# Self-attention's first stretch of a fused four-layer kernel, in halves of 512 tokens: second projection in two other banks, value products moved up, rows of ones filled by ScalarE

## What is computed

```python
def _mha(xk, xv, xq, Wk, Wv, Wq, Wo, bo, masked):        # 16 heads of 16
    K = jnp.einsum('bse,hed->bhsd', xk, Wk)
    V = jnp.einsum('bse,hed->bhsd', xv, Wv)
    Q = jnp.einsum('bqe,hed->bhqd', xq, Wq)
    scores = jnp.einsum('bhqd,bhkd->bhqk', Q, K)
    scores = jnp.where(causal, -jnp.inf, scores)
    att = jax.nn.softmax(scores / jnp.sqrt(sk), axis=-1)
    out = jnp.einsum('bhqk,bhkd->bhqd', att, V)
    ...
x = x + tanh(g_xattn[2]) * _L2_xattn_ref(_layernorm(x), ctx, ...)   # a = _mha(inputs, inputs, inputs, ..., masked=True) first
```

## Time and profile before

| | us |
|---|---|
| median of 3 runs | 2710.25 |
| lowest, highest | 2708.65, 2712.22 |
| the profiled execution | 2702.28 |
| its span, first to last instruction | 2700.5 |
| self-attention's stage begins | 1039.4 |
| its first peak product | 1078.75 |
| its maxima turned (L3168) | 1092.1 |
| first unit of batch 0 (L3235) | 1096.0 |

### The profile page before, as it was taken

One profiled execution on the slowest core, in us unless ns is written; L12 is line 12 of the kernel. 1 busy time (PEld: TensorE's weight loads), 2 busy tenths in 40 slices (PEclk: granted clock), 3 DMA queues, 4 the chain that ended last, 5 costly groups with the idle time before them and its releaser, 6 DMA issues. The chain is left out here.

```text
span 2700.5 us, 43042 instructions
## 1 busy us (share of the span) xinstructions
PE 2420.3 (90%) x12786; PEld 1429.2 (53%) x12787; DVE 1612.7 (60%) x3262; ACT 1288.6 (48%) x2559; POOL 1351.7 (50%) x2270
## 2 busy tenths in 40 slices
PE   6997999999996775799999999899969975999997
PEld 3554666766663553344445344355546663666664
DVE  5884664655554874687877868488866644212121
ACT  4664443544443773466566566566653431222221
POOL 3665663233445774224353434466875304656663
PEclk9998999999998998899999999999988986999999
DMA  4001000000100003222141231100004151222222
GB/s 137 6 1 67 1 0 1 1 0 1 47 1 16 1 0 76 62 66 71 31 111 44 54 87 37 48 24 24 1 1 164 47 197 24 45 46 47 43 47 28
DMA packets 85449, 115.14 MB, mean 43 GB/s; under 512 B 15432, under 2 KB 64432, under 8 KB 83600
## 3 DMA queue, kind: packets, MB, share of 16 engines
q1 hardware_dynamic: 66736, 92.36, 11.4%
q0 software_dynamic: 18528, 20.50, 4.7%
HBM read 77.92 MB, written 34.64 MB: 42 GB/s over the span
## 5 line engine op out<-in xcount | busy, mean ns | idle before, releaser
L3411 ACT ACTIVATE L2S_pT<-L2S_t_ps 128x512 f32<-128x512 f32 (+3 forms) x768 | 356.2, 491 | 212.8 <-PE L2S_t_ps L3235 204.3
L3475 DVE TENSOR_REDUCE L2S_mx<-L2S_s_ps 128x1 f32<-128x768 f32 (+7 forms) x384 | 350.5, 951 | 111.0 <-PE L2S_s_ps L3158 110.2
L3235 PE MATMUL L2S_t_ps<-L2S_q,L2S_k 98*128 98x512 bf16 (+3 forms) x768 | 248.4, 334 | 16.3 <-DMA L2S_q<-L2S_mrow 6.4
L3715 POOL TENSOR_SCALAR_AFFINE_SELECT L2S_pT<-L2S_pT 128x128 f32<-128x128 f32 x512 | 150.8, 309 | 170.0 <-ACT L2S_pT L3411 165.6
L3157 PE MATMUL L2S_s_ps<-L2S_k,L2S_q 96*128 96x512 bf16 (+3 forms) x768 | 198.5, 331 | 16.3 <-DVE L2S_mx L3475 7.5
L622 POOL TENSOR_TENSOR L_prob<-L_prob,L_rc 128x616 f32<-128x616 f32 x64 | 82.2, 1285 | 231.5 <-DVE L_rc L555 231.5
L4091 DVE TENSOR_TENSOR L3B_h<-L3B_si,L3B_u_ps 128x512 f32<-128x512 f32 x71 | 48.9, 688 | 237.4 <-PE L3B_u_ps L4034 237.4
L4008 POOL DMA_INDIRECT out<-L3B_y,L3F_rows x71 | 114.7, 1616 | 134.6 <-DVE L3B_y L4097 120.1
L3235 PEld LDWEIGHTS L2S_t_ps<-L2S_q,L2S_k 98*128 98x128 bf16 x768 | 72.8, 97 | 194.9 <-ACT L2S_pT L3411 129.0
L3335 PE MATMUL L2S_o_ps<-L2S_pT,L2S_v 128*32 128x512 f32 (+3 forms) x1536 | 165.4, 504 | 0.0
L319 PE MATMUL L_scores<-weights,L_xT 128*128 128x308 f32 x512 | 143.2, 423 | 2.3 <-ACT L_xT L442 1.6
(11 more groups left out here) (540 smaller groups left out, 5803.0 us busy)
## 6 DMA issues: line engine op xcount, KB each, us to landing
qk_parts<-L2S_part SPq DMA_DIRECT2D x90, 128.0 KB, 2.4
L2S_q<-qk_parts SPq DMA_DIRECT2D x32, 192.0 KB, 3.4
L2S_k<-qk_parts SPq DMA_DIRECT2D x30, 192.0 KB, 3.4
L2S_q<-qk_parts SPq DMA_DIRECT2D x32, 128.0 KB, 3.2
L3F_w<-in_L_gu SPq DMA_DIRECT2D x8, 512.0 KB, 6.9
weights<-in_L_w SPq DMA_DIRECT2D x8, 512.0 KB, 9.0
out<-x_sb SPq DMA_DIRECT2D x8, 512.0 KB, 3.3
expert_rows<-L_xn SPq DMA_DIRECT2D x8, 512.0 KB, 3.0
```

The source lines that it names most:

```text
L3235: nc.tensor.matmul(o[:, lo:512], k6[:, q % 2, j, kt * P:(kt + 1) * P], q6[:, q % 2, c, j, lo:512], start=True, stop=True).then_inc(s["t_fu ...
L3411: nc.scalar.activation(pT[:, st % SLOTS, j, lo:512], t_ps[j % 2][:, lo:512], ACT.Exp, scale=SK).then_inc(s["exp_done"], 1)
L3475: nc.vector.tensor_reduce(dst, src, AX.X, ALU.max).then_inc(s["mx_done"], 1)
L3715: nc.gpsimd.affine_select(out=edge, in_=edge, compare_op=ALU.is_ge, fill=0.0, base=0, pattern=[[1, P]], channel_multiplier=-1).then_inc(s[ ...
```

## The change

- `turn_x`, and `project(m)` for both m, go by halves c of 512 tokens: PE turns tiles 0 to 3 when these four are normalised, then tiles 4 to 7; ACT copies halves; PE projects, in this order, low queries, low keys, high queries, high keys, each half into one bank; ACT and DVE split halves (128x512 in place of 128x1024, twice as many).
- The second projection (m = 1) goes to `o_ps` (queries) and `r_ps` (keys), which nobody else uses yet, so it no longer waits for `s_ps`. Its low halves are made before the first peak, its high halves after peaks 2 and 3. `turn_max` on PE now also waits until the last rest has left `r_ps`.
- `first_v` of tiles 0 to 3 comes ahead of the second projection; tiles 4 and 5 come after peaks 0 and 1, tiles 6 and 7 after peaks 4 and 5.
- SP writes the low queries of quad 0, then of quad 1; when quad 0's have landed it reads them back, and then writes the low keys of quad 1 and the high queries. The high queries of quad 0 and quad 1's queries and keys are read later. POOL writes quad 0's low keys and reads them back as soon as these three have landed; then it writes the high keys of both quads and reads the high half back. Quads 0 and 1 take 24 writes of half the size in place of 12.
- The rows of ones in `k6` are filled by ACT as its first instruction in the stage, in place of POOL.
- ACT overwrites a high part of m = 0 in a half only when that half's writes have landed. `rest_done`, `act_pre` and `pre_full` are counted anew.

Names of semaphores and their setup are left out of the diff, and context lines.

```diff
@@ -2987,12 +2987,21 @@
...
-    turn_x()
-    project(0)
-    project(1)
+    for c in range(2):
+        turn_x(c)
+    for c in range(2):
+        for f in range(2):
+            project(0, c, f)
+    for t in range(4):
+        first_v(t)
+    for f in range(2):
+        project(1, 0, f)
     for n in range(TB):
         peak(0, n)
-        first_v(n)
+        if n in (2, 3):
+            project(1, 1, n - 2)
+        if n in (0, 1, 4, 5):
+            first_v({0: 4, 1: 5, 4: 6, 5: 7}[n])
...
@@ -3038,6 +3047,9 @@
...
+def projected(m, c, f):
+    return (o_ps, r_ps)[f][:] if m else s_ps[f][:, c * 512:(c + 1) * 512]
+
...
@@ -3086,14 +3098,35 @@
...
-        write(0, 0, 0, 2)
+        lows, highs = part[:, 0, :, lowc], part[:, 0, :, highc]
+        sp.wait_ge(s["split_low"], 1)
+        for qq, sem in ((0, "q_first"), (1, "q_rest")):
+            for p in range(3):
+                sp.dma_start(dram["parts"][0:1, qq, p, :, :, lowc].rearrange("o d h s -> (o d) h s"),
+                             lows[64 * qq:64 * qq + 64, p, :]).then_inc(s[sem], 16)
+        sp.wait_ge(s["q_first"], 48)
+        chip.settle(sp)
+        load(0, 0, "q", lowc, s["loaded_low0"])
+        sp.wait_ge(s["split_low"], 2)
+        for p in range(3):
+            sp.dma_start(dram["parts"][1:2, 1, 2 - p, :, :, lowc].rearrange("o d h s -> (o d) h s"),
+                         part[64:128, 1, p, lowc]).then_inc(s["k_rest"], 16)
+        sp.wait_ge(s["split_done"], 2)
+        for p in range(3):
+            for qq in range(2):
+                sp.dma_start(dram["parts"][0:1, qq, p, :, :, highc].rearrange("o d h s -> (o d) h s"),
+                             highs[64 * qq:64 * qq + 64, p, :]).then_inc(s["written0"], 16)
+        sp.wait_ge(s["written0"], 96)
+        chip.settle(sp)
+        load(0, 0, "q", highc, s["loaded_high0"])
+        sp.wait_ge(s["q_rest"], 48)
+        for n in ("k_first", "k_rest"):
+            sp.wait_ge(s[n], 48)
         sp.wait_ge(s["k_written"], 96)
         sp.sem_inc(s["written1"], 96)
-        written(0, 0)
-        for q in range(2):
-            for cols, n in ((lowc, "low"), (highc, "high")):
-                for which in "qk" if q else "q":
-                    load(0, q, which, cols, s[f"loaded_{n}{q % 2}"])
+        for cols, n in ((lowc, "low"), (highc, "high")):
+            for which in "qk":
+                load(0, 1, which, cols, s[f"loaded_{n}1"])
...
@@ -3168,28 +3201,27 @@
...
-        def turn_x():
-            pe.wait_ge(s["xn_done"], TB)
+        def turn_x(c):
+            pe.wait_ge(s["xn_done"], 4 * c + 4)
             for dh in range(KD):
-                for i in range(TB):
+                for i in range(4 * c, 4 * c + 4):
...
-        def project(m):
-            if m == 0:
-                pe.wait_ge(s["act_pre"], 2)
-            else:
-                pe.wait_ge(s["rest_done"], 2)
-            for f in range(2):
-                for c in range(2):
-                    for k in range(KD):
-                        mm = nc.tensor.matmul(s_ps[f][:, c * 512:(c + 1) * 512], w[("L2S_Wq", "L2S_Wk")[f]][:, k, m * P:(m + 1) * P],
-                                              xT[:, k, c * 512:(c + 1) * 512], start=(k == 0), stop=(k == KD - 1))
-                mm.then_inc(s["pre_full"], 1)
+        def project(m, c, f):
+            if not m:
+                pe.wait_ge(s["act_pre"], 2 * c + 2)
+            elif c:
+                pe.wait_ge(s["rest_done"], 5 + f)
+            o = projected(m, c, f)
+            for k in range(KD):
+                mm = nc.tensor.matmul(o, w[("L2S_Wq", "L2S_Wk")[f]][:, k, m * P:(m + 1) * P],
+                                      xT[:, k, c * 512:(c + 1) * 512], start=(k == 0), stop=(k == KD - 1))
+            mm.then_inc(s["pre_full"], 1)
...
-                pe.wait_ge(s["act_pre"], 6 + t // 2 - 1)
+                pe.wait_ge(s["act_pre"], 9 + (t - 4) // 2)
...
@@ -3205,12 +3237,13 @@
...
+            pe.wait_ge(s["rest_done"], 8)
...
-        pe.wait_ge(s["act_pre"], 10)
+        pe.wait_ge(s["act_pre"], 16)
...
@@ -3375,24 +3408,27 @@
...
-        def turn_x():
+        nc.scalar.activation(k6[KR:MR].rearrange("p a h s -> p (a h s)"), wide(chip.neghalf[KR:MR, 0:1], [MR - KR, 8 * S]), ACT.Copy,
+                             scale=0.0, bias=1.0).then_inc(s["k_ones"], 1)
+
+        def turn_x(c):
             for f in range(2):
-                act.wait_ge(s["pre_full"], f + 1)
-                copy(xT[:, f, :], s_ps[f][:], "act_pre")
-
-        def project(m):
-            for f in range(2):
-                act.wait_ge(s["pre_full"], 2 * m + f + 3)
-                if m:
-                    act.wait_ge(s[f"written{f}"], m * 96)
-                copy(part[:, f, 0, :], s_ps[f][:], "act_pre")
+                act.wait_ge(s["pre_full"], 2 * c + f + 1)
+                copy(xT[:, f, c * 512:(c + 1) * 512], s_ps[f][:, c * 512:(c + 1) * 512], "act_pre")
+
+        def project(m, c, f):
+            act.wait_ge(s["pre_full"], (5, 11)[m] + (2, 3)[m] * c + f)
+            if m:
+                for n, count in (((("q_first", 48), ("q_rest", 48)), (("k_first", 48), ("k_rest", 48))), ((("written0", 96),), (("k_written", 96),)))[c][f]:
+                    act.wait_ge(s[n], count)
+            copy(part[:, f, 0, c * 512:(c + 1) * 512], projected(m, c, f), "act_pre")
...
-                act.wait_ge(s["pre_full"], 7 + g)
+                act.wait_ge(s["pre_full"], (9, 10, 13, 16)[g])
...
@@ -3509,18 +3545,15 @@
...
-        def project(m):
-            for f in range(2):
-                n = 2 * m + f + 1
-                dve.wait_ge(s["act_pre"], 3 + 2 * m + f)
-                dve.wait_ge(s["split_done"], n)
-                nc.vector.tensor_tensor(first_rest[:, f, :], s_ps[f][:], part[:, f, 0, :], ALU.subtract).then_inc(s["rest_done"], 1)
-                dve.wait_ge(s["rest_done"], n)
-                if m:
-                    dve.wait_ge(s[f"written{f}"], m * 96)
-                nc.vector.tensor_copy(part[:, f, 1, :], first_rest[:, f, :]).then_inc(s["mid_done"], 1)
-                dve.wait_ge(s["mid_done"], n)
-                nc.vector.tensor_tensor(part[:, f, 2, :], first_rest[:, f, :], part[:, f, 1, :], ALU.subtract).then_inc(s["split_done"], 1)
+        def project(m, c, f):
+            n = 4 * m + 2 * c + f + 1
+            cols, mid, split, number = slice(c * 512, (c + 1) * 512), ("mid_low", "mid_done")[c], ("split_low", "split_done")[c], 2 * m + f + 1
+            dve.wait_ge(s["act_pre"], (5, 11)[m] + (2, 3)[m] * c + f)
+            nc.vector.tensor_tensor(first_rest[:, f, cols], projected(m, c, f), part[:, f, 0, cols], ALU.subtract).then_inc(s["rest_done"], 1)
+            dve.wait_ge(s["rest_done"], n)
+            nc.vector.tensor_copy(part[:, f, 1, cols], first_rest[:, f, cols]).then_inc(s[mid], 1)
+            dve.wait_ge(s[mid], number)
+            nc.vector.tensor_tensor(part[:, f, 2, cols], first_rest[:, f, cols], part[:, f, 1, cols], ALU.subtract).then_inc(s[split], 1)
...
@@ -3677,27 +3710,32 @@
...
-            nc.gpsimd.memset(k6[KR:MR], 1.0).then_inc(s["k_ones"], 1)
-            pool.wait_ge(s["k_ones"], 1)
...
-        def project(m):
-            if m:
+        def project(m, c, f):
+            if m or not f:
                 return
-            pool.wait_ge(s["split_done"], 3)
+            cols = slice(c * 512, (c + 1) * 512)
+            pool.wait_ge(s[("split_low", "split_done")[c]], 2 + c)
             chip.settle(pool)
-            for p in range(3):
-                for qq in range(2):
-                    nc.gpsimd.dma_start(dram["parts"][1:2, qq, 2 - p, :, :, :].rearrange("o d h s -> (o d) h s"),
-                                        part[64 * qq:64 * qq + 64, 1, p, :]).then_inc(s["k_written"], 16)
-            pool.wait_ge(s["k_written"], 96)
+
+            def k_out(qq, sem):
+                for p in range(3):
+                    nc.gpsimd.dma_start(dram["parts"][1:2, qq, 2 - p, :, :, cols].rearrange("o d h s -> (o d) h s"),
+                                        part[64 * qq:64 * qq + 64, 1, p, cols]).then_inc(s[sem], 16)
+
+            k_out(0, ("k_first", "k_written")[c])
+            if c:
+                k_out(1, "k_written")
+                pool.wait_ge(s["k_written"], 96)
+            else:
+                pool.wait_ge(s["k_first"], 48)
             chip.settle(pool)
             src = dram["parts"][1:2]
-            for cols, n in ((slice(0, S // 2), 0), (slice(S // 2, S), 1)):
-                for slot, count, p in ((0, 3, 0), (3, 2, 1), (5, 1, 2)):
-                    nc.gpsimd.dma_start(k6[slot * HD:(slot + count) * HD, 0, :, cols],
-                                        src[:, 0, p:p + count, :, :, cols].rearrange("o p d h s -> (o p d) h s")).then_inc(s[f"k_loaded{n}"], 16)
+            for slot, count, p in ((0, 3, 0), (3, 2, 1), (5, 1, 2)):
+                nc.gpsimd.dma_start(k6[slot * HD:(slot + count) * HD, 0, :, cols],
```

(1 more changed line is left out.)

6 lines of the change are left out of this document (3 added, 3 removed).

## The result

The changed kernel takes 2697.38 us (median of 8 runs, 2694.89 to 2702.51). The kernel before took 2707.57 beside it (median of 8, 2704.50 to 2712.22). The ratio of the two kernels is 0.9969, 95% interval 0.9959 to 0.9979: 8.4 us less, between 5.7 and 11.1. The two medians lie 10.2 us apart. The forecast was 2703.1 with a range of 2699.5 to 2707.5. Its sign was right; the measured time lies 2.1 us under the range.

What follows compares the result with a forecast made beforehand. The bound was the serial chain from the stage's beginning through the keys' write and read to the peaks: 10.5 us gained, 3.3 lost, 7.1 by the turned maxima. Off the 2710.25 median this gave 2703.1, range 2699.5 to 2707.5.

Steps and rivals of the forecast that it cites:

- The chain is thus xn, PE, ACT, DVE, a write, a read, PE: Stage beginning to first peak: a serial path without parallel work, so each microsecond saved there counts in the whole time.
- POOL's first write: Quad 0's low keys: POOL begins writing near 1058.0 us, with the stage beginning at 1039.4; before, 1065.21.
- DVE's order at the peaks: Among quad 0's peaks: peak 2, high queries' split, peak 3, high keys' split, then peaks 4 to 7.
- The rule on small transfers: Quad 0's writes: about 2.0 us fixed each, so halving them buys nothing; landing halved with bytes would gain 1.2 us more.
- the difference is taken off the median: 2703.1: Whole kernel: the gain of 7.1 us taken off the median of the runs shown, 2710.25 us.
- I take 4.4, the middle: Third read of quad 0's low keys: landing between bounds of 3.4 and 5.4 us, first peak at 1068.3.
- The stretch is 16.7 us in place of 13.4: First peak to turned maxima: two half splits on DVE and the half clock lose 3.3 us, bounds 1.5 and 5.
- From turned maxima to the first unit nothing changes, 3.9 us: The maxima's way through POOL after the peaks: 3.9 us as before, no loss.
- The late read: Rival, chance 0.18: keys' read lands in about 8 us, first peak 1072, gain 3.6, time 2706.6.
- The fill was not slow: Rival, chance 0.05: ACT's fill of ones takes 14 us, 5.3 late, gain 1.8, time 2708.4.
- Batch 0's first 30 us: Slower rival, chance 0.05: clock at 0.50 after the first unit loses 4 to 12 us; 2715 at 12.
- Splits hidden, clock full: Rival, chance 0.12: half splits slip under PE, full clock at the peaks; loss 0 to 1, gain 10, 2700.2.

Runs made afterwards that it cites:

- e8_late_keys: Changed kernel, but POOL writes no keys until all four halves are split, then writes all nine pieces before reading back; 2706.92 us, ratio to the kernel before 0.9997.
- e7_whole_norm: Changed kernel, but PE starts its first four transposes only when all eight tiles are normalised; 2698.97 us (one run).
- six variants named under e7: Six variants of the changed kernel with early transposes, a late clock rise and no fill on POOL; POOL's first write at 18.8 to 19.1 us after stage start.
- e12: The changed kernel itself measured once more, nothing altered; 2696.41 us (12 runs), ratio to the kernel before 0.9972.
- e11_reads_together: Changed kernel, but SyncE reads quad 0's low queries back only when POOL's low-key writes have landed, so both reads start together; 2698.84 us (one run).
- e5_splits_late: Changed kernel, but the second projection's high halves and their splits stand behind quad 0's turned maxima; 2694.53 us (5 runs), ratio to the kernel before 0.9948.
- e10: e5_splits_late, but SyncE also holds quad 1's high-half reads until quad 0's turned maxima have landed; 2691.61 us (9 runs), ratio to the kernel before 0.9947.
- e4: Changed kernel, but SP holds back the twelve writes of quads 2 and 3 until the two rows of maxima have landed; 2695.60 us (one run).
- e1: Changed kernel, but POOL fills the rows of ones again after the norm, as before; 2702.45 us (one run).

## Why the prediction was right and where it failed

**Right: the path and the order of things.** "The chain is thus xn, PE, ACT, DVE, a write, a read, PE": e8_late_keys shows its write and read, e7_whole_norm its beginning. One reading in it was incomplete: before, the queries' read ended PE's wait, 0.5 us behind the keys'. The steps, forecast against measured: ACT's fill 7.0 and 7.02; POOL's first write S+18.6 and S+17.7 (S+18.8 to 19.1 in the six variants named under e7); last write's issue to the first read's 3.5 and 3.4 (1060.89 to 1064.25); DVE's order at the peaks as written, with peak 3 between the splits.

**The rule on small transfers.** Writes of 64 KB landed in 2.1 us (three of SyncE's, 1059 to 1062 us) and 2.3 us (POOL's), where one of 128 KB took 2.5. Half the bytes saved 0.2 to 0.4 us, not 1.2. The Trainium skill, page "DMA: Bandwidth & Descriptors", section "Anatomy of one DMA — SWDGE (gpsimd) path", has it so for transfers that POOL issues, with about 2.0 us fixed; this trace agrees (2.3 us for POOL's, where the estimate was 2.15). Six of SyncE's writes of 64 KB beside POOL's low reads, issued from 1064 to 1067 us, took 3.1 us.

**Failed: the base.** The step "the difference is taken off the median: 2703.1" took 2710.25, a median of 3 runs, for the kernel's time. It was 2707.57, 2707.84 and 2707.16 in groups of 8 to 20 runs (the first group holds the three), some 2.7 us lower. The measured 2697.38 lies 5.7 us under the forecast: 2.7 of these are the base, and 3.0 the gain, which was 7.1 in the forecast and is 10.2 between the two medians (10.8 in e12). By the ratios the gain is 8.4 and 7.6 us, and 7.1 lies inside both intervals (5.7 to 11.1; e12: 4.1 to 11.1). With the base of 8 runs the same sum gives 2700.4, and the range, moved as far, reaches down to 2696.8, below the measured time. With the measured gain and the old base it would have been 2700.1, inside the range as well. So the time left the range because both went the same way, and the range held nothing for the base, though 2702.28 for the profiled execution had shown 8 us of spread. The terms of the gain that were off follow.

**Mis-sized: the read of the keys.** "I take 4.4, the middle" was a mean of two rows that stood for two different situations. The read took 3.3 us, 1.1 less; e11_reads_together shows why. The reason given for the 4.4, that half-size writes now run beside it, was not what counted: they did run beside it. The working itself had SyncE's queries "read back by 1061.0, earlier than the keys"; the row of a single read, 3.4, was the one that answered to that.

**Mis-sized: the peaks.** "The stretch is 16.7 us in place of 13.4": measured 15.4 (after, e12), 13.7 where the clock held. I had put the half clock over 4.46 us as before; it was 0.62 over the 4.5 us, so the high queries' split ended 8.8 us after the first peak and not 9.5. From there to the end of the high keys' split it was 2.4 us in place of 2.6, and from there to the turned maxima 4.2 in place of 4.6. The loss against before is 2.0 us in place of 3.3.

**Small and against it: the last step.** "From turned maxima to the first unit nothing changes, 3.9 us": 4.6, as the maxima's transfers now met a share of 0.92 and landed in 2.1 us, not 1.6. The same term, harmless here, then ate 4 us in e5_splits_late.

In the profiled execution, counted from S: first peak 12.3 gained (forecast 10.5), stretch 2.0 lost (3.3), last step 0.7 lost (0): 9.6 for 7.1. Of the 1.8 more at the first peak, 1.1 is the read and most of the rest the earlier write (S+17.7 for S+18.6), which came with the clock's early rise and only where the stage began late. That part is luck of the execution: in time from the program's start the first unit came 7.3 us earlier, not 9.6.

**The rivals.** The late read did not come (3.3 us, not 8). The fill was not slow. Batch 0's first 30 us had PE busy 22.3 us at 0.78, 0.83 and 0.66, about as before, and batch 1's first maxima were sent 156.0 us after the first unit (155.8 before), so batch 0 gave back no more than 0.2 us. "Splits hidden, clock full", 2700.2, was half true: the splits were not hidden, the clock was full in some executions.

## What to carry to other kernels

When two chains through memory meet at one consumer, start them apart: the third reads here took 3.0 us (queries) and 3.3 us (keys) apart and 5.4 and 5.5 together, for the same bytes. Before moving work off a path look at what the small transfer at its end will find in flight; holding six reads, 0.8 MB that nobody needed yet, for 5 us turned 1 us of gain at the first unit into 5 in the profile, of which batch 0 gave 1.1 back. And a base from three runs is an unknown like any other: it needs its own width in the range.

## What the runs showed of the hardware

- Two transfers of 4 KB landed in 1.6 us with the transfer engines at a share of 0.02 to 0.11 (e10, before), in 2.1 at 0.57 (e4, reads ahead) and at 0.92 (changed kernel, writes ahead), in 4.2 at 1.11 (e1) and in 6.1 at 1.14 (e5). They took 1.6 us in e8 too, at 0.48 with three writes ahead, so the share alone does not tell. The 4 KB were the same each time; what differed was what was in flight ahead of them.
- A read of 64 KB on POOL's queue, behind two larger ones, took 3.1 to 3.5 us in ten kernels with writes beside it, and 5.2 to 5.5 us in four with reads on SyncE's queue beside it.
- DVE's 128x512 cast took 0.68 us while POOL was filling two rows of 8192 values, and 0.43 us for the next half, with POOL idle (e1_pool_fill).
- PE's granted clock rose 2.8 to 3.0 or 5.0 to 5.6 us after the same first transposition, in kernels whose PE had the same instructions up to there, and fell behind an idle time of 2.3 to 2.5 us (changed, e12, e7) or did not behind 2.2 and 2.6 us (e4, e1): 15.4 or 13.7 us for the same eight peaks. Differences of 1 to 2 us between two profiled executions at such a place say nothing of the kernels.
- An ACT copy on 2 partitions with a source of one repeated value costs what its length costs: 7.02 us for 8192 values, where 1024 and 512 values on 128 partitions took 1.02 and 0.60 us.
